# Expert chunks packed by a plan made on the chip, weights loaded per chunk, row buffers three deep

## The reference

```
x = layernorm(x + attention(x))                  # x: (32, 512, 256) f32, 16 heads
logits = x @ Wg.T                                # N = 16384 tokens, E = 8 experts
top_v, top_i = top_k(logits, 2); gates = softmax(top_v)
pos_f = running count of each expert's tokens, in order of tokens
keep = pos_f < cap                               # cap = N*2*1.25/8 = 5120
h = exp_batches @ W1                             # W1: (8, 256, 1024)
h = gelu(h[:, :512]) * h[:, 512:]
exp_out = h @ W2                                 # W2: (8, 512, 256)
out = segment_sum(where(keep, gate, 0) * exp_out[of the pair], token)
x = layernorm(x + out)
```

## Time and profile before

| | us |
|---|---|
| median of 3 runs | 3489.76 (3483.92 to 3495.27) |
| the profiled execution's own time | 3492.51 |
| its span in the trace | 3490.8 |
| PE busy | 3226.1 (92%) |
| DVE busy | 2446.6 (70%) |
| ACT busy | 2113.1 (61%) |
| POOL busy | 1755.3 (50%) |

### The profile page before, as it was taken

One profiled execution on the slowest core, in us unless ns is written; L12 is line 12 of the kernel. 1 busy time (PEld: TensorE's weight loads), 2 busy tenths in 40 slices (PEclk: granted clock), 3 DMA queues, 4 the chain that ended last, 5 costly groups with the idle time before them and its releaser, 6 DMA issues. The chain is left out here.

```text
span 3490.8 us, 65927 instructions
## 1 busy us (share of the span) xinstructions
PE 3226.1 (92%) x22018; PEld 2115.3 (61%) x22018; DVE 2446.6 (70%) x5673; ACT 2113.1 (61%) x4197; POOL 1755.3 (50%) x1501
## 2 busy tenths in 40 slices
PE   5999999999999999999999599999999999999960
PEld 3444444444444445444444288888888888888850
DVE  4888888888888888888887364545455545454439
ACT  2788888888877787878886444444444444444420
POOL 5356565656556565656562343434353534353334
PEclk7999999999999999999998799999999999999985
DMA  2455555433333333333332244434345434442439
GB/s 87 142 160 173 160 173 160 123 87 98 87 97 82 97 88 98 87 96 91 92 94 65 77 75 63 74 58 77 57 68 78 62 61 62 70 61 43 62 73 338
DMA packets 397883, 339.88 MB, mean 97 GB/s; under 512 B 257720, under 2 KB 315456, under 8 KB 397632
## 3 DMA queue, kind: packets, MB, share of 16 engines
q1 hardware_dynamic: 334656, 252.20, 27.8%
q0 software_dynamic: 58368, 67.74, 11.3%
q10 hardware_dynamic: 4608, 16.78, 1.2%
HBM read 89.92 MB, written 152.17 MB: 69 GB/s over the span
## 5 line engine op out<-in xcount | busy, mean ns | idle before, releaser
L974 DVE TENSOR_REDUCE peak<-ps 128x1 f32<-128x512 f32 x2048 | 1338.5, 683 | 293.0 <-PE ps L654 292.4
L749 ACT ACTIVATE probs<-ps 128x512 f32<-128x512 f32 x2048 | 1124.5, 611 | 173.8 <-PE ps L664 164.9
L1163 POOL DMA_INDIRECT x<-out,token x320 | 501.7, 1568 | 800.0 <-ACT out L1249 669.4
L1193 PE MATMUL ps_hid<-x_hi,stack 128*128 128x512 f32 x2560 | 804.2, 395 | 30.9 <-DVE x_lo L1286 26.3
L664 PE MATMUL ps<-stack 50*128 50x512 f32 x2048 | 786.2, 453 | 3.4 <-DVE peak L974 2.7
L654 PE MATMUL ps<-stack 48*128 48x512 f32 x2048 | 753.8, 446 | 18.9 <-DMA stack<-qk_lo 13.6
L1292 DVE TENSOR_TENSOR hid<-ps_hid,act_in 128x512 f32<-128x512 f32 x320 | 219.1, 689 | 598.0 <-ACT act_in L1235 597.8
L654 PEld LDWEIGHTS ps<-stack 48*128 48x128 f32 x2048 | 336.0, 189 | 466.7 <-issue 223.2
L1193 PEld LDWEIGHTS ps_hid<-x_hi,stack 128*128 128x128 f32 x2560 | 476.5, 188 | 140.3 <-DVE x_lo L1286 26.4
L680 PE MATMUL ps_pv<-probs,v 128*17 128x512 f32 x4096 | 546.9, 606 | 1.2 <-ACT probs L749 1.2
L1193 PE MATMUL ps_hid<-x_lo,stack 128*128 128x512 f32 x1280 | 505.4, 395 | 0.0
(11 more groups left out here) (136 smaller groups left out, 4095.6 us busy)
## 6 DMA issues: line engine op xcount, KB each, us to landing
stack<-qk_hi SPq DMA_DIRECT2D x1024, 64.0 KB, 2.3
expert_rows<-blank SPq DMA_DIRECT2D x80, 520.0 KB, 4.0
quarters<-expert_rows SPq DMA_DIRECT2D x320, 128.0 KB, 2.7
stack<-qk_lo SPq DMA_DIRECT2D x512, 64.0 KB, 2.3
xs<-in_L_attn_x SPq DMA_DIRECT2D x32, 512.0 KB, 4.3
x<-row SPq DMA_DIRECT2D x32, 512.0 KB, 3.3
fy<-x SPq DMA_DIRECT2D x32, 512.0 KB, 4.6
out<-fz ACTq DMA_DIRECT2D x32, 512.0 KB, 4.7
```

The costliest lines, as they stand in the source:

```text
L749: act.activation(probs[:, j % RING, :], ps[it.bank(("cols", s * UNITS + j))][:], ACT.Exp, scale=SCALE).then_inc(s_exp, 1)
L974: dve.tensor_reduce(peak[s % 2][:, u:u + 1], ps[it.bank(("rows", n))][:], AX.X, ALU.max, negate=True).then_inc(s_max, 1)
L1163: pool.indirect_dma_start(x1_dram, bass.IndirectOffsetOnAxis(ap=token[buf][:, t:t + 1], axis=0), out[buf][:, t, :], None, bounds_check=n_t ...
L1193: last = pe.matmul(ps_hid[f % 2][:, part, :], w[c.par][k][:, cols], xx[c.odd][:, k, :], start=i == 0, stop=i == 3 * KT - 1)
```

## The change

- **Plan.** At the end of attention a matmul of `ones` and `carry` gives each expert's count to all partitions. DVE computes from it, in some 70 small instructions, which chunks hold rows: `plan.numbers[0]` is the place in the table of each unit and `plan.numbers[1]` its expert. There are 72 units: 63 whole ones of 512 slots and 9 half ones of 256 slots. Units without rows take a blank place, one chunk of blank rows that is added at the end of the table, and are computed like the others.
- **Weights per unit.** Every unit has its own weights: SP reads the expert from the plan and loads `w1` and `w2` for each of the 72 units. The units alternate between the two sets of split weights. ACT rounds them (three more instructions per unit), DVE makes the remainder of `w1` (two more), POOL that of `w2` (one).
- **Rows** have three buffers instead of two.
- **Straight code.** The units are unrolled; the hardware loops of `experts` are gone.

The edits, cut to what counts:

```diff
-        def load_rows(odd, n): ...
-            def body(k):
-                if k.lead and k.odd and not k.final_expert:
-                    wait(sp, s_w, k.e * W_PIECES)
-                    weights.load(sp, k.e + 1, s_raw)
-                if not k.last:
-                    sp.wait_ge(s_turn, k.n * KT + KT)
-                    sp.wait_ge(s_meta, k.n + 1)
-                    load_rows(k.odd, k.n + 2)
+            def load_rows(n):
+                x_rows, meta = rows_of[plan.tiles(n)]
+                rows = plan.rows(sp, n)           # value_load(numbers[0:1, 0, n])
+                for a in range(QUARTERS):
+                    sp.dma_start(quarters[n % RING_X][a * BLOCK:(a + 1) * BLOCK, 0:cols(n) // BLOCK],
+                                 x_rows[rows, a]).then_inc(s_rows[n % RING_X], 16)
+                sp.dma_start(meta_rows[n % RING_X][:, 0:plan.tiles(n)], meta[rows]).then_inc(...)
+            for n in range(RING_X):
+                load_rows(n)
+            expert = plan.weights(sp, 1)          # value_load(numbers[0:1, 1, n])
+            sp.wait_ge(s_w1, KT)
+            weights.load_w1(sp, expert)
+            for n in range(n_units):
+                if n + RING_X < n_units:
+                    sp.wait_ge(s_turn, n * KT + KT)
+                    sp.wait_ge(s_meta, n + 1)
+                    load_rows(n + RING_X)
+                if n + 2 < n_units:
+                    later = plan.weights(sp, n + 2)
+                    sp.wait_ge(s_w1, (n + 2) * KT)
+                    weights.load_w1(sp, later)
+                if n + 1 < n_units:
+                    sp.wait_ge(s_w2, n + 1)
+                    weights.load_w2(sp, expert)
+                    expert = later
```

```diff
         # GpSimd
-                    for i, (raw, hi, lo) in enumerate(weights.pieces(1 - k.par)):
-                        pool.tensor_copy(hi, raw).then_inc(s_whi, 1)
-                        pool.wait_ge(s_whi, k.e * W_PIECES + (i + 1))
-                        pool.tensor_tensor(lo, raw, hi.bitcast(F32), ALU.subtract).then_inc(s_w, 1)
+            def low_w2(n):
+                pool.wait_ge(s_whi2, n + 1)
+                pool.tensor_tensor(w2_lo[n % 2], raw2, w2_hi[n % 2].bitcast(F32), ALU.subtract).then_inc(s_w2, 1)
+            low_w2(0)
+            for n in range(n_units):
+                if n + 1 < n_units:
+                    low_w2(n + 1)
+                pool.wait_ge(s_scaled, scaled_before(n + 1))
+                wait(pool, s_add, added_before(n))
+                for t in range(plan.tiles(n)): ...   # the indirect DMAs into x1
         # ScalarE, unit n (high_x, gelu, high_h, scale as before)
+                high_x(n + 1); gelu(n, 0); gelu(n, 1); high_h(n, 0)
+                high_w1(n + 1, 0)                    # waits s_raw1, w1 of unit n+1
+                high_h(n, 1)
+                high_w1(n + 1, 1)
+                high_w2(n)                           # waits s_raw2, w2 of unit n
+                scale(n - 1); gelu(n, 2); gelu(n, 3); high_h(n, 2); high_h(n, 3)
         # VectorE, unit n
+                turn(n + 1); low_x(n + 1); product(n, 0); product(n, 1); low_h(n, 0)
+                low_w1(n + 1, 0)
+                low_h(n, 1)
+                low_w1(n + 1, 1)
+                meta(n); product(n, 2); product(n, 3); low_h(n, 2); low_h(n, 3)
         # TensorE, unit n
+                pe.wait_ge(s_w1, (n + 1) * KT)
+                pe.wait_ge(s_xlo, n * KT + KT)
+                hidden(n, 0); hidden(n, 1)
+                output(n - 1)                        # also waits s_w2 >= n
+                hidden(n, 2); hidden(n, 3)
```

```diff
         # end of attention, SP
-                    if s == 3 and it.known and b == n_seq:
-                        sp.wait_ge(s_pv, n_seq * UNITS)
-                        weights.load(sp, 0, s_raw)
+            sp.dma_start(table_rows[EXPERTS * per], blank...)   # the blank chunk
+            sp.wait_ge(s_pv, n_seq * UNITS)
+            sp.wait_ge(s_planned, 2)
+            first = plan.weights(sp, 0)
+            weights.load_w1(sp, first)
+            weights.load_w2(sp, first)
```

More of the change, by code:

```diff
@@ L222, in __init__, with load_w1, load_w2, rows @@
         self.w2_rows = w2.rearrange("e (k p) d -> e p k d", p=P)
-    def load(self, engine, e, s_raw):
+    def load_w1(self, engine, e):
         for a in range(QUARTERS):
[L226 to L236, removed]
+            engine.dma_start(self.raw1[a * BLOCK:(a + 1) * BLOCK], self.w1_rows[e, a]).then_inc(self.s_raw1, 16)
+    def load_w2(self, engine, e):
+        engine.dma_start(self.raw2, self.w2_rows[e]).then_inc(self.s_raw2, 16)
+class Plan:
+    def __init__(self, sb, n_tokens, cap):
+        self.per = cap // SEQ
+        self.blank = EXPERTS * self.per
+        halves = n_tokens * TOPK // (SEQ // 2) + EXPERTS - 1
+        self.whole = (halves - EXPERTS) // 2
+        self.n_halves = halves - 2 * self.whole
+        self.n_units = self.whole + self.n_halves
+        self.n_chunks = self.whole + (self.n_halves + 1) // 2
+        self.numbers = sb("plan_numbers", [P, 2, self.n_units], U32)
+        self.expert = sb("plan_expert", [P, self.n_units])
+    def rows(self, engine, n):
+        last = self.blank if n < self.whole else 2 * self.blank + 1
+        return engine.value_load(self.numbers[0:1, 0, n:n + 1], min_val=0, max_val=last)
+    def weights(self, engine, n):
+        return engine.value_load(self.numbers[0:1, 1, n:n + 1], min_val=0, max_val=EXPERTS - 1)
+    def tiles(self, n):
+        return TILES if n < self.whole else TILES // 2
+    def tiles_before(self, n):
+        return sum(self.tiles(i) for i in range(n))
+def attention(nc, x, w_qkv, w_proj, b_proj, w_gate, x1_dram, table, stacks, probs, weights, plan):
     n_seq = x.shape[0]
-    cap = table.shape[0] // EXPERTS
+    cap = (table.shape[0] - SEQ) // EXPERTS
     per = cap // SEQ
@@ L326, in attention @@
         token = sb("token", [P, TILES])
+        steps = sb("steps", [P, per])
+        chunk_no = sb("chunk_no", [P, plan.n_chunks])
+        half_no = sb("half_no", [P, plan.n_halves])
         s_const = sem("s_const")
@@ L1019, in _, with planned, then @@
             iterations(dve, n_seq, body)
[L1020 to L1037, removed]
+            def planned(ins):
+                ins.then_inc(s_plan, 1)
+                step[0] += 1
+            def then():
+                dve.wait_ge(s_plan, step[0])
@@ new lines, in _ @@
+            total = work([P, EXPERTS])
+            reached = work([P, EXPERTS, per])
+            own_chunks = work([P, EXPERTS])
+            own_steps = work([P, EXPERTS])
+            small = work([P, EXPERTS])
+            small_at = work([P, EXPERTS])
+            upto = work([P, 2 * EXPERTS, EXPERTS])
+            ends = work([P, 2 * EXPERTS])
+            ended = work([P, plan.n_chunks, EXPERTS])
+            start = work([P, plan.n_chunks])
+            chunk_e = work([P, plan.n_chunks])
@@ new lines, in _ @@
+            then()
+            planned(dve.tensor_reduce(own_chunks, reached, AX.X, ALU.add))
+            then()
+            planned(dve.tensor_tensor(small, own_steps, own_chunks, ALU.subtract))
+            then()
+            for e in range(EXPERTS):
+                planned(dve.tensor_copy(upto[:, e, 0:e + 1], own_chunks[:, 0:e + 1]))
+                planned(dve.tensor_copy(upto[:, EXPERTS + e, 0:e + 1], small[:, 0:e + 1]))
+            planned(dve.scalar_tensor_tensor(small_at, number[:], float(per), own_chunks, ALU.mult, ALU.add))
@@ new lines, in _ @@
+            then()
+            planned(dve.tensor_reduce(ends, upto, AX.X, ALU.add))
+            then()
+            planned(dve.tensor_tensor(ended, spread(ends[:, 0:EXPERTS], C), widen(chunk_no[:], EXPERTS), ALU.is_le))
+            then()
+            planned(dve.tensor_reduce(chunk_e, ended, AX.X, ALU.add))
+            then()
+            planned(dve.tensor_tensor(ended, ended, spread(ends[:, 0:EXPERTS], C), ALU.mult))
+            dve.tensor_copy(plan.expert[:, 0:W], chunk_e[:, 0:W]).then_inc(s_planned, 1)
@@ new lines, in _ @@
+            dve.tensor_scalar(plan.numbers[:, 1, 0:W], chunk_e[:, 0:W], EXPERTS - 1.0, None, ALU.min).then_inc(s_planned, 1)
+            then()
+            planned(dve.tensor_reduce(start, ended, AX.X, ALU.max))
+            planned(dve.scalar_tensor_tensor(place, chunk_e, float(per), chunk_no[:], ALU.mult, ALU.add))
+            then()
+            planned(dve.tensor_tensor(place, place, start, ALU.subtract))
+            then()
+            planned(dve.tensor_scalar(place, place, float(plan.blank), None, ALU.min))
@@ new lines, in _ @@
+            then()
+            planned(dve.tensor_reduce(small_e, by_small, AX.X, ALU.add))
+            planned(dve.tensor_scalar(is_small, is_small, -1.0, 1.0, ALU.mult, ALU.add))
+            then()
+            for i in range(H):
+                c = slice(W + i // 2, W + i // 2 + 1)
+                planned(dve.tensor_scalar(half_place[:, i:i + 1], place[:, c], 2.0, float(i % 2), ALU.mult, ALU.add))
```

(100 more changed lines are left out.)

265 lines of the change are left out of this document (155 added, 110 removed).

## The result

The changed kernel takes 3478.38 us (median of 7 runs, 3470.35 to 3483.93), the kernel before 3490.57 in 7 runs beside it: ratio 0.9962, interval 0.9947 to 0.9977. So it is 12 us faster here; 3437, or 53 less, had been forecast. The profiled execution took 3483.93 us, its span is 3482.2.

The account below looks back on a forecast made before the run. PE bounds the kernel before; after the change the `w1` round trip was to set the pace. Units 1315.2 against 1364.3 us (-49.1), edges -4.0: 3439.4 profiled, 3437 as median; range 3320 to 3515.

Parts of the forecast that it names:

- What bounds the kernel before, and the saving: `experts` is bound by PE, busy 1356.67 of 1365 us; after the change PE alone would need 1146.2 us, 210.6 less.
- The loop: In `experts`, the round trip between landings of `w1`: 18.2 us per whole unit, above PE's 16.96, and 17.9 per half.
- Steps 1 to 3: From `w1` landed, through its split and `meta` held 2.40 us behind POOL's `low_w2`, to SP's next issue: 7.26 us.
- Step 4: In SP's queue, rows of unit n+3, then `w1` of n+2: 9.9 us from first row issue to last `w1` landing.
- rival on the other side: The round trip in `experts` is longer than the chunks saved: at 19.3 us per unit +26, 3513 us; chance 0.18.
- Step 5: SP's two value loads per unit, place of the rows and expert: 0.5 us each, 1.0 together, bounds 0.1 and 4.6.
- the forecast's own formula: Experts' stage: 63 x 18.2 + 9 x 17.9 + 7.5 = 1315.2 us against 1364.3, so 49.1 less.
- The end: After the last unit, a half: two of four indirect DMAs and two scales fall away, 4.5 us less.
- The rival that PE keeps the pace: In whole units `meta` gets through before `low_w2`, the loop is 15.8 us and PE's 16.96 counts: 3337 us; chance 0.22.

## Why the prediction was wrong

**What bounds the kernel before, and the saving:** right. With `w1` first the stage is 1168.6 us, 195.7 less than before, against a limit of 210.6 by PE's pace.

**The loop:** right in kind. One raw buffer, split, `meta` behind POOL, rows and then `w1` behind `meta` in SP's queue. Three experiments took a piece out of the circle each, and each let the period fall to what was left or to PE's 16.96; taking away PE's work did not.

**Steps 1 to 3:** 7.4 us measured against 7.65 at the same points. The reading that the waiting POOL instruction goes first held: the gate instruction took 2.3 to 2.4 us instead of 0.22 in 57 of the 63 whole units (mean 2145 ns), and in five of the other six one of the two small instructions of `meta` behind it was held as long.

**Step 4 failed:** `w1` lands 8.07 us after its first issue and not 7.15. This is the term that was mis-sized. I took 9.9 between bounds of 9.9 and 11.1 because one load of the trace of before had it. Its last landing came 6.9 us after the first `w1` issue (the sum made it 7.06), while the seven loads of `w1` inside `experts` took 6.7 to 8.0 us for this, 7.26 in the mean (from their issues and landings in that trace). That is 0.2 of the 0.92. For the rest the adds are to blame. In six of the seven they begin 1.0 to 1.9 us after `w1`'s first issue (the seventh, the first of the stage and the slowest, has none near it); now, in every unit, they begin about 1 us ahead of the rows and over 4 us ahead of `w1` (POOL's first add at 2524.45, `w1` from 2528.74 in the round above). The prediction itself said in its rival on the other side that the adds would start with the rows, and left it out of the sum. The run without the adds has 7.30, which is 0.77 less and the mean of before again. That their earlier start is what counts is argued and not shown.

**Step 5:** 1.0 us forecast for two value loads; the two gaps they lie in are together 0.3 longer than forecast, and removing them takes 1.65 out, with register work. The loads by themselves were sized nearly right, 0.56 to 0.58 us each against 0.5; the register work ahead of the issues, which constants save as well, was for the most part already in the rows of before that the sum used. In the changed kernel's trace the 72 loads of a place took 263 to 282 ns, the register operation behind each 152 to 174 and the range check 18.

**The size:** 63 x (19.07 - 18.2) = 55 us more than forecast. With the forecast's own formula 19.07 would even have been 10 us slower than before: the period lies in the range of the rival on the other side, whose point of equality was 18.9. (For P = 19.3 that rival's +26 makes 3516, not 3513.) It came out faster because of two errors the other way, so that the sign agrees with the forecast is luck. The halves in the loop took 18.3 us (109.6 us from the output of unit 63 to that of unit 69, counted from 0), but the last two took 10.5 and 7.8: nothing is left to load for them. So the 9 halves and the edges of the stage cost 152.7 us instead of 168.6. The end was 6.5 us shorter instead of 4.5. The last stage took 7.6 us more, which nothing in the prediction covers. Together: -53.1 + 54.8 - 15.9 - 2.0 + 7.6 = -8.6, the profiled difference.

**The rival that PE keeps the pace** (3337) needed `meta` ahead of `low_w2`; moving that work to DVE shows what it is worth: 1196.0 us, where that rival said 1215.5.

**DVE's stall behind POOL** came in nearly every unit: GpSimd's subtraction held DVE's gate instruction for 2 us (mean 2145 ns, against 220 with that subtraction on DVE). It made 158 us or more where it lay in the loop (1354.1 and 1360.9 us against 1196.0), and nothing that can be told where it did not (1168.6 us with it, 1172.3 without). The traces show that the two end together, at 2524.29 and 2524.32 in the round above; what makes DVE wait is not shown.

## What to carry to other kernels

When loads become more frequent, draw the circle from landing to the next landing through every queue it passes, before adding up busy time: no engine was busy all the time here (PE 918 of 1000 us), DMA's share was 0.66 where 0.79 was reached with `w1` first, and the pace was still not PE's. In an in-order queue, issue the load that has a single buffer ahead of the load that has three; that order alone was worth 186 to 192 us (1354.1 and 1360.9 against 1168.6). A landing time should be taken from all loads of its kind and not from one (here 7.26 us in the mean and 6.9 in the one), and raised when other transfers will now start ahead of it in every unit (8.07 us with the adds, 7.30 without them).

## What was not expected of the hardware

- Four indirect adds per unit made the median landing of a 512 KB load 7.6 to 8.6 us instead of 6.3.
- DMA's share did not tell whether loads set the pace. It was 0.66 when loads set the pace and 0.79 when PE did.
- The last stage's 512 KB loads landed in 6.2 us instead of 4.8 after a change that does not touch that stage, on the same chip.
- Attention took 244 to 278 us more on two of the chips, while the changed kernel's experts' stage differed by 7 us.
